# A fused perceiver layer: the last gate group by silu, one step for the exponential's bias, and reordered stages

## The reference, cut to what matters

```python
x = x + xattn(layernorm(x), ctx)          # x: 128 sequences of 32 rows, 256 wide; ctx: 257 rows each
x = x + mixer(layernorm(x))               # in_proj, 3-tap conv, silu -> u; x_proj, softplus -> delta; a scan; out_proj
x = x + ffn(layernorm(x))

# xattn: attn = softmax((q @ k.T) / 16); out = (x + attn @ v) @ Wo.T + bo
# mixer: state = exp(delta * A) * state + delta * u * B over 32 positions, 512 channels, 16 states; y = sum(state) + u * D
# ffn:   xq = round(x * 127 / max|x|) etc. (8 bit rows, ternary weights)
#        h = silu(xq @ w_gate.T) * (xq @ w_up.T);  hq = round(h * 127 / max|h|) etc.;  out = hq @ w_down.T
```

## Time and profile before

| | us |
|---|---|
| median of 3 runs | 1031.91 |
| lowest and highest run | 1031.90, 1033.83 |
| the profiled execution, its own time | 1036.67 |
| the span of that execution in its trace | 1034.5 |
| busy PE, DVE, ACT, POOL in the span | 925.0, 894.5, 756.4, 852.8 |

### The profile page before, as it was taken

The page is one execution under the profiler, slowest core; times in us unless marked ns, Lnnn a source line. Parts: engine busy times, 40 slices in busy tenths (PEclk is TensorE's granted clock), DMA queues, the critical chain, the costliest instruction groups (busy, mean ns, idle before and its releaser), DMA issues. The chain is left out here.

```text
span 1034.5 us, 13058 instructions
## 1 busy us (share of the span) xinstructions
PE 925.0 (89%) x4158; PEld 488.3 (47%) x4192; DVE 894.5 (86%) x1216; ACT 756.4 (73%) x1323; POOL 852.8 (82%) x616
## 2 busy tenths in 40 slices
PE   8886988999989999899989999899989999867896
PEld 6642453545435453545435454545435454423454
DVE  1635888899989999899989999899989999899965
ACT  2356657877797859877797859877797869666555
POOL 1059998899979898899979898898979898899920
PEclk9998989999999999999999999999999999989999
DMA  9804710445042610545043610535033400500000
GB/s 354 333 34 163 289 59 2 162 147 202 0 150 99 243 42 2 183 143 205 0 128 115 246 44 2 184 125 223 2 109 120 161 0 2 184 0 0 1 21 21
DMA packets 21915, 116.33 MB, mean 112 GB/s; under 512 B 3479, under 2 KB 4119, under 8 KB 9304
## 3 DMA queue, kind: packets, MB, share of 16 engines
q1 hardware_dynamic: 16232, 80.70, 21.2%
q10 hardware_dynamic: 5616, 34.81, 9.4%
HBM read 111.04 MB, written 4.46 MB: 112 GB/s over the span
## 5 line engine op out<-in xcount | busy, mean ns | idle before, releaser
L1172 DVE TENSOR_TENSOR_SCAN state<-decay,state 128x512 f32<-128x512 f32 (+1 forms) x352 | 590.5, 1696 | 35.3 <-ACT decay L932 22.8
L861 POOL TENSOR_TENSOR state<-w,brep 128x512 f32<-128x512 f32 (+1 forms) x352 | 612.5, 1771 | 0.5 <-POOL w L894 0.4
L1326 PE MATMUL acc<-state,ident 128*128 128x512 f32 x832 | 412.3, 612 | 15.7 <-DVE state L1172 13.8
L932 ACT ACTIVATE decay<-delta,neg_a 128x496 f32<-128x496 f32 x512 | 329.6, 669 | 89.7 <-DVE state L1172 88.6
L1326 PEld LDWEIGHTS acc<-state,ident 128*128 128x128 f32 x832 | 148.5, 193 | 165.5 <-issue 111.9
L869 POOL TENSOR_TENSOR state<-state 128x512 f32<-128x512 f32 x96 | 122.2, 1273 | 45.8 <-DVE state L1172 44.3
L1326 PE MATMUL bank<-xn_t,in_w 128*128 128x512 f32 x128 | 62.0, 618 | 5.0 <-DVE u L1318 3.4
L1326 PE MATMUL bank<-out_w,u 128*128 128x256 f32 x256 | 58.2, 383 | 8.7 <-DVE u L1159 8.7
L916 ACT ACTIVATE soft<-x_in,nmr,rstd 128x256 f32<-128x256 f32 x64 | 33.2, 589 | 42.9 <-POOL nmr L825 42.9
L966 ACT ACTIVATE sg<-bank,ag 128x512 f32<-128x512 f32 x64 | 43.6, 681 | 24.0 <-PE bank L1326 23.1
L894 POOL TENSOR_TENSOR w<-delta,u 128x512 f32<-128x512 f32 x32 | 39.9, 1269 | 22.7 <-ACT delta L1068 22.7
(11 more groups left out here) (170 smaller groups left out, 1318.2 us busy)
## 6 DMA issues: line engine op xcount, KB each, us to landing
keys<-in_keys_t SPq DMA_DIRECT2D x32, 1028.0 KB, 6.0
brep<-b_scratch ACTq DMA_DIRECT2D x32, 1024.0 KB, 6.8
keys<-in_keys_n SPq DMA_DIRECT2D x29, 1024.0 KB
out<-x_in SPq DMA_DIRECT2D x16, 256.0 KB, 5.0
x_in<-in_x SPq DMA_DIRECT2D x14, 256.0 KB
u<-in_keys_n SPq DMA_DIRECT2D x1, 1024.0 KB
w<-in_keys_n SPq DMA_DIRECT2D x1, 1024.0 KB
delta<-in_keys_n SPq DMA_DIRECT2D x1, 1024.0 KB
```

Of the source, the lines that this page charges most:

```text
L861: nc.gpsimd.tensor_tensor(state[g % CPT][:, 0:count * tok].rearrange("p (c t) -> p c t", c=count), w[:, m, 0:tok].unsqueeze(1).to_broadcas ...
L932: last = nc.scalar.activation(decay[:, q:q + groups * GSEQ, 1:LEN], d, ACT.Exp, scale=neg_a[:, m, n + i:n + i + 1])
L1172: nc.vector.tensor_tensor_scan(flat, by, flat, 0.0, ALU.mult, ALU.add).then_inc(scan_done, 1)
L1326: return nc.tensor.matmul(o, l, r, start=first, stop=last)
```

## The change

1. With a scan, halves 0 to 5 go by tanh as before; halves 6 and 7 (group 3) take `ACT.Silu` at L966 and `gate` is left out for them (`BY_TANH = 3`). `ag` then needs gate/2 for three groups and gate for the fourth, from a small table `gate_step`; `hs` gets the factor of `ag` for three groups only.
2. `-SCALE` (-1/16) is multiplied into the query weights, their bias, `kb_col` and `kb_const` once, in `qk`. `s_max` becomes a minimum, `s_neg` falls away, `s_bias` is one instruction ebias = (mx + kb) - kb, and the exponential has scale -1.
3. The tables `SECOND`, `PRE`, `PRE_END`, `POST_FIRST` and `POST` get other steps. `FIRST` and `POST_END` change only by the parts that fall away, `LAST` and `TAIL` not at all.

```diff
+BY_TANH = 3
...
 PRE = [
-    ("s_neg", [14, 17, 27, 35]),
-    ("s_max", [14, 16, 26, 34]),
-    ("s_bias", [14, 19, 27, 38]),
-    ("exp", [13, 20, 28, 38]),
-    ("stats1", [1]),
-    ("stats2", [52]),
-    ("u_evac", [58, 59, 64, 64]),
-    ("silu", [61, 67, 67, 67]),
-    ("dt", [72, 72, 85, 86]),
-    ("b_load", [80, 82, 85, 87]),
-    ("softplus", [83, 87]),
+    ("s_max", [14, 20, 25, 33]),
+    ("s_bias", [15, 21, 26, 34]),
+    ("exp", [15, 21, 28, 35]),
+    ("stats1", [0]),
+    ("stats2", [51]),
+    ("u_evac", [60, 62, 63, 66]),
+    ("silu", [62, 67, 67, 67]),
+    ("dt", [76, 79, 87, 87]),
+    ("b_load", [75, 80, 87, 87]),
+    ("softplus", [84, 87]),
...
 POST = [
-    ("x_max", [9]),
-    ("tanh", [14, 16, 19, 24, 41, 46, 58, 68]),
-    ("gate", [15, 17, 19, 28, 43, 45, 57, 68]),
-    ("hidden", [16, 18, 20, 30, 43, 50, 63, 69]),
-    ("up", [10, 14, 17, 23, 37, 44, 51, 65]),
-    ("h_max", [19, 31, 54, 71]),
-    ("finish", [31, 63, 77, 86]),
+    ("x_max", [12]),
+    ("tanh", [14, 17, 20, 25, 49, 53, 62, 68]),
+    ("gate", [16, 18, 22, 29, 50, 53]),
+    ("hidden", [16, 18, 22, 30, 51, 56, 64, 67]),
+    ("up", [10, 13, 17, 23, 37, 52, 59, 65]),
+    ("h_max", [20, 31, 59, 71]),
+    ("finish", [31, 66, 77, 83]),
...
 POST_END = [
-    ("gate", [16, 18, 25, 27, 49, 53, 58, 67]),
+    ("gate", [16, 18, 25, 27, 49, 53]),
...
-                                             ACT.Tanh if scan else ACT.Silu,
+                                             ACT.Tanh if scan and g < 2 * BY_TANH else ACT.Silu,
...
-                                             bias=ebias[:, g:g + 1], scale=SCALE,
+                                             bias=ebias[:, g:g + 1], scale=-1.0,
...
-                nc.vector.tensor_copy(qk_w[:, :, :].rearrange("p h d -> p (h d)"), bank[:, A, :])
-                nc.vector.tensor_copy(q_bias[:, :], acc[:, 0:HALVES])
...
+                    last = nc.vector.tensor_scalar(to, of, -SCALE, None, ALU.mult)
...
+                link(nc.vector.tensor_scalar(gate_step[:, :], ones[:, 0:GROUPS], ffn_s[:, 0:1], None, ALU.mult))
+
+                link(nc.vector.tensor_scalar(gate_step[:, BY_TANH:GROUPS], gate_step[:, BY_TANH:GROUPS], 2.0, None, ALU.mult))
...
-                            nc.vector.tensor_scalar(ag[:, n], low, ffn_s[:, 0:1], None, ALU.mult)\
+                            nc.vector.tensor_tensor(ag[:, n], low, gate_step[:, n], ALU.mult).then_inc(alphas_ready, 1)
...
-                        nc.vector.tensor_scalar(nmx[:, one], mx[:, one], kb[:, one], -SCALE, ALU.add, ALU.mult)\
-                            .then_inc(nmax_done, 1)
...
+                        nc.vector.scalar_tensor_tensor(ebias[:, one], mx[:, one], kb[:, one], kb[:, one],
+                                                       ALU.add, ALU.subtract).then_inc(ebias_ready, 1)
...
-                    after(pe, gated, b, halves)
+                    after(pe, gated, b, min(halves, 2 * BY_TANH))
+                    if halves > 2 * BY_TANH:
+                        reach(pe, gate_tanh, b, halves)
```

More of the change, by code:

```diff
@@ L158 @@
[L158 to L161, removed]
+    ("q_evac", [12]),
+    ("query", [3]),
+    ("rstd1", [0]),
+    ("times_u", [80, 82, 87, 87]),
+    ("stats2", [52]),
+    ("softplus", [80, 85]),
+    ("rstd2", [51]),
+    ("p_turn", [16, 26, 31, 36]),
+    ("z_turn", [22, 29, 33, 41]),
+    ("s_max", [15, 18, 26, 29]),
+    ("evac2", [56]),
+    ("turn1", [0]),
+    ("z_evac", [23, 29, 33, 41]),
+    ("tap2", [64, 64, 69, 70]),
@@ new lines @@
+    ("stats1", [0]),
+    ("x_dbl", [75]),
+    ("p_sum", [19, 20, 32, 41]),
+    ("s_bias", [15, 18, 26, 29]),
+    ("xn2", [53]),
+    ("b_load", [80, 84, 87, 87]),
+    ("tap0", [63, 63, 67, 69]),
+    ("dt", [70, 70, 78, 81]),
+    ("xn1", [5]),
+    ("u_evac", [62, 64, 67, 69]),
+    ("add2", [82]),
+    ("x_proj", [69]),
+    ("p_evac", [18, 27, 32, 37]),
+    ("p_last", [17, 22, 28, 35]),
+    ("score", [7, 18, 23, 28]),
+    ("turn2", [55]),
+    ("zt_evac", [26, 30, 35, 43]),
+    ("silu", [65, 66, 69, 70]),
@@ new lines @@
+    ("s_max", [14, 20, 25, 33]),
+    ("dt", [76, 79, 87, 87]),
+    ("turn2", [56]),
+    ("times_u", [82, 82, 87, 87]),
+    ("attend", [19, 27, 32, 40]),
+    ("rstd1", [0]),
+    ("p_evac", [18, 28, 32, 37]),
+    ("u_evac", [60, 62, 63, 66]),
+    ("z_turn", [24, 28, 33, 44]),
+    ("z_evac", [21, 29, 34, 43]),
+    ("score", [5, 14, 23, 27]),
+    ("zt_evac", [26, 31, 36, 44]),
+    ("turn1", [3]),
+    ("rstd2", [52]),
+    ("stats1", [0]),
+    ("add1", [46]),
+    ("x_proj", [68]),
+    ("mix_in", [58, 58, 59, 61]),
@@ new lines @@
+    ("b_load", [75, 80, 87, 87]),
+    ("p_turn", [14, 25, 31, 37]),
+    ("evac2", [56]),
+    ("x_dbl", [71]),
+    ("add2", [61]),
+    ("query", [3]),
+    ("p_sum", [20, 24, 32, 43]),
+    ("tap2", [59, 61, 65, 65]),
+    ("xn2", [53]),
+    ("softplus", [84, 87]),
+    ("attn_out", [46, 46]),
+    ("s_bias", [15, 21, 26, 34]),
+    ("xn1", [6]),
+    ("q_evac", [9]),
+    ("x1", [49, 51]),
+    ("exp", [15, 21, 28, 35]),
+    ("stats2", [51]),
+    ("evac1", [7]),
+    ("p_last", [16, 23, 28, 36]),
@@ new lines @@
+    ("h_evac", [32, 35, 74, 80]),
+    ("h_max", [20, 31, 59, 71]),
+    ("down", [32, 63, 76, 82]),
+    ("xn3", [9]),
+    ("x_turn", [7]),
+    ("h_turn", [29, 33, 72, 77]),
+    ("h_floor", [22, 32, 63, 74]),
+    ("rstd3", [3]),
+    ("tanh", [14, 17, 20, 25, 49, 53, 62, 68]),
+    ("finish", [31, 66, 77, 83]),
+    ("x2", [3, 5]),
+    ("hidden", [16, 18, 22, 30, 51, 56, 64, 67]),
+    ("h_scale", [24, 32, 65, 74]),
+    ("up", [10, 13, 17, 23, 37, 52, 59, 65]),
+    ("scale_h", [26, 33, 70, 76]),
```

214 lines of the change are left out of this document (65 added, 149 removed).

## The result

The changed kernel is slower, and its time scatters. Six runs lie between 1041.15 and 1070.7 us with a median of 1057.07, beside 1032.96 for the kernel before (six runs, 1031.9 to 1034.09). The ratio is 1.0157, 95% interval 1.0094 to 1.022. This interval is from the shorter runs alone, and the profiled execution (1066.98 us) is one of the longer ones. The forecast was 1020.1.

A forecast was written before the change was run, and what follows sets the result against it. In full phases DVE was taken to bound before `stats2` and ACT after it, POOL in phase 1. Terms 6 x -1.75, -0.7, -0.4, -0.2 gave -11.8 us, from 1031.91 to 1020.1; 80% range 1012 to 1030.

The forecast's parts named there:

- the paragraph on `s_neg`: Before `stats2`: dropping four `s_neg` a phase saves 0.6 us, less waits between dependent instructions, net -0.4 us a phase.
- The sum of a full phase: DVE's stretch before `stats2` shortens by 1.75 us a phase, giving scan to scan distance near 114.7 us.
- Two gates, -1.2: Half 5's gate and hidden move behind `stats2` into the room of gates 6 and 7: -1.2 us a phase.
- `x_max`, -0.65: Before `stats2`: `x_max` three steps later ends DVE's wait for ACT's normed rows, -0.65 us a phase.
- `y` at slot 22, -0.5: Before `stats2`: most of DVE's 0.71 us wait for PE at slot 22 goes, -0.5 us a phase.
- Exponential of group 3 ahead of scan 19, +0.8: Exponential and `p_last` on ACT now stand ahead of scan 19's decays, delaying DVE by 0.8 us a phase.
- The +0.2 for the bare scans: Five scans follow bare on DVE; a two-state decay is longer than a one-state scan: +0.2 us a phase.
- ACT's stretch, 0: From `stats2` on, where ACT sets the pace: no change, between -0.5 and +1.9 us.
- Rival C: Half 6's load and silu delay the mixer's chain before `u_evac` 1: slower than before, about 1037 us; chance 0.09.
- The last scan phase, -0.7: Final scan phase: -1.2 us for two gates, about +0.5 for two late decays at separate silu visits.
- Once, -0.4: Opening: block 0's four `s_neg` stand in a chain there, so leaving them out saves 0.4 us.
- phase 1, -0.2: Phase without FFN, bound by POOL: the new `SECOND` table gives -0.2 us, within 2 either way.

The follow-up runs named there:

- experiment 8: Two kernels on experiment 5's: the first with the table `SECOND` as before, 1023.1 us; the second with `stats1` at step 1 instead of 0, 1027.26 us.
- experiment 2: Changed kernel with the bias's minimum written to and read from a PSUM column, same two-tensor form: 1030.45 us, ratio 0.9975.
- experiment 5: Experiment 1's kernel with `hs` rewritten so that no small VectorE instruction has two SBUF tensor inputs: 1026.57 us, ratio 0.9937.
- experiment 6: Experiment 1's kernel with all eight halves by tanh and the gates of halves 6 and 7 back on VectorE: 1034.83 us, ratio 1.0007.
- experiment 7: Experiment 8's first kernel with the bias made in two one-input VectorE instructions again: 1030.72 us against 1023.1.
- experiment 4: Both code edits with old steps: 1047.58 us; half 6's silu at 61: 1066.17; also experiment 5's edit: 1067.69; also `down` at 63, `finish` at 66: 1036.98.
- experiment 1: Changed kernel with the bias as `tensor_scalar`, `kb` a per-partition scalar and only `mx` a tensor input: 1030.23 us, ratio 0.9942.

## Why the prediction was wrong, point by point

**The step that failed** is the paragraph on `s_neg`: it put a net gain of 0.4 us a phase on four instructions fewer, with the new `s_bias` at what the old one took. The new one is of another form. It has two tensor inputs in SBUF, and one such instruction cost up to 7.9 us. In place of -0.4, four of the six full phases became 5.1 to 6.1 us longer and the last one 4.4 (it ends 1.7 us early, since no block's `stats1` stands at its end); in the first the second group's bias got in after 0.55 us. In the phase at 433.5 the piece up to scan 26 is 73.6 us, beside 65.9 without the instruction (experiment 8), and the four two-input instructions in it take 7.3 us more than they would with POOL idle. No rival had it, so the range had no room for it either. The rows could have bounded it: POOL is busy 104.9 us of a full phase, and none of DVE's instructions in the earlier trace rows has two tensor inputs in SBUF (`sg` has one in PSUM, `nmx` and `ebias` take their second operand as a scalar). An instruction whose like the rows don't show should have carried a bound of its own, up to POOL's longest row of work.

**The sum of a full phase came out once that was away, in part by luck.** It said about 114.7 us. Experiments 2, 5 and 8 show 114.8 to 114.9 where the clock holds, and DVE busy 108.3 us, as predicted. But scan 19 was put 0.57 us too high, and a wait of gate 0 that it didn't have is 0.57 us longer than before; these two cancel. Its terms:

- *Two gates, -1.2:* 1.55 us, by experiment 6. But the reason was wrong. I had DVE's room behind `stats2` at 4.6 us and took a gate there as nearly free; cut at scans 26 and 35 the trace of the kernel before has 1.6 us of room in that piece, and the new one 1.7. The 4.6 were the sum over two pieces.
- *`x_max`, -0.65:* right, the wait is gone (446.43, no idle ahead of it). *`y` at slot 22, -0.5:* right in kind, 0.7 us are gone.
- *`s_neg`, -0.4:* with a one-input bias it is 1.1 us, by experiment 7 and as placed there.
- *Exponential of group 3 ahead of scan 19, +0.8:* mis-sized, the wait is 0.23 us. Its bias comes early enough in one step. The +0.2 for the bare scans behind it is right (0.23, at 495.42 in the changed kernel).
- *Not foreseen:* gate 0 waits 0.65 us for its tanh; in the kernel before it was under 0.1 in most phases.
- *ACT's stretch, 0:* right (26.6 and 26.6). Rival C's mechanism is real, though not where it put the price: experiment 4 has PE held up 3.85 us by half 6's silu, and full phases 4.5 to 6.1 us longer than with `down` moved. The move of `down` to 63, which I had passed over, is what prevents it.

**The last scan phase, -0.7:** it takes 99.3 us in experiments 1, 5 and 8's second kernel, 98.9 in its first, where it was 99.0. In other traces the granted clock of this phase is lower (0.915 or 0.916 instead of 0.931) and it takes longer: 100.9 in the changed kernel, 100.4 with tanh and gates (experiment 6), 101.9 in experiment 2. So the two detours eat what the two gates give, by this comparison perhaps 0.5 us more. 65 table loads, as predicted. The activation starts 1.29 us after its load here as before.

**Once, -0.4, and phase 1, -0.2:** the opening gives 1.5 us (first scan at 83.8 instead of 85.3; 85.4 again with the bias in two steps), and phase 1 loses 1.3 with the new steps (109.4 in experiment 5) and gains 0.7 with the old.

**From 1020.1 to 1026.6** (experiment 5): the span in its trace is 1026.2 us, 3.5 over the 1022.7 that my sum gives from the span before. Phase 1 is 1.5 us and the last scan phase 1.0 us worse than I said, the first full phase 0.6 us worse (115.3), phases 3 to 6 together 1.9 us, of which 1.2 are the clock (two falls there, one in the kernel before); the last full phase is 0.4 us better though the clock falls in it, the opening 1.2 us better. The other 3 us are no mechanism: I took the runs' median to be 4.8 us below the profiled execution, and here it is 1.4 below (1028.0). That the change as it stands is slower is all the two-input instruction: its median falls from 1057.07 to 1030.23 us with that instruction's inputs read in another way.

## What to carry to other kernels

When a fused form replaces two small instructions, look where every operand lies, not only at the count. With GpSimd near 90% busy, a VectorE instruction with two tensor inputs in SBUF waits for it, even if it is one column wide; a pointer scalar or an input in PSUM does the same arithmetic without the wait. And when a bank's reader moves to a later step on one engine, move the matmul that needs the bank behind it too, since everything queued behind that matmul waits with it.

## What the runs showed of the hardware that I had not expected

- A VectorE instruction with two SBUF tensor inputs can be passed over: it missed up to six boundaries between GpSimd instructions in a row (11.35 us), and once it had missed one, only a pause of GpSimd let it in. At boundaries behind a pair sum it was never passed over (31 of 31), between two products 10 times of 17.
- The granted clock of TensorE can fall from 2.4 to 1.2 GHz for some 3.4 us in one phase and not in the one before it, with the same busy time of PE ahead of it (7.34 of 7.5 us in both). It costs 1.2 us a phase here. Five such phases or none are, as an estimate, 6 us, about the scatter in experiments 1 and 5 (1022.9 to 1031), and there the runs with the higher mean clock are the shorter ones (in experiment 1 0.984 for 1022.89, 0.970 to 0.973 for those over 1030). What sets it off stays open.
